# Dense filler products on TensorE in two context attentions: one per two half steps, twelve at the beginning

## The chip, the cores and the metric

The kernel runs on one core of a Trainium2 chip. The metric is the device time of one execution in microseconds; three executions give a median of 5088.73 us. The core has a matrix engine (TensorE, PE in the rows; its weight loads are PEld), VectorE (DVE), ScalarE (ACT), GpSimd (POOL) and a queue engine (SP) that issues DMAs. They run side by side and meet at semaphores.

## What is computed

A decoder of four layers over x (4 batches, 512 tokens, 128 features) and a context of 154 tokens. Each layer has a self attention, an attention to the context and a feed-forward part; after each comes a residual sum and a layer norm. The change touches the context attentions of layers 0 and 1 (16 heads of 8 features). Layer 0:

```python
Q, K, V = (proj(q, w_q), proj(k, w_k), proj(v, w_v))
scores = jnp.einsum('bhqd,bhkd->bhqk', Q, K) / jnp.sqrt(jnp.float32(D_K))
keep = (mask != 0)[:, None, None, :]
scores = jnp.where(keep, scores, NEG)
attn = jax.nn.softmax(scores, axis=-1)
x = jnp.einsum('bhqk,bhkd->bhqd', attn, V)
```

Layer 1 first picks for each query the context token with the best score, and attends over the picked tokens (a token picked several times counts as often):

```python
idx = jnp.argmax(scores, axis=-1)
mem = jnp.take_along_axis(kv, idx[..., None], axis=1)
...
attn = jax.nn.softmax(logits, axis=-1)
out = jnp.einsum('bhlm,bmd->bhld', attn, mv)
```

In the kernel the mask of the first, and the never-picked tokens of the second, are a key bias: one more row of the key stack (`key_bias`). The causal attention of layer 1 and the context attention of layer 2 use masks and no key bias, the differential attention of layer 2 neither; all go through the same function.

## The kernel before

`attend` (L496) does all heads of one attention. Its main loop has N = 32 slots, one for a pair of heads of a batch; two slots are a quad. A context attention has four half steps in a slot, numbered k = 0, 1 (outer) and i = 0, 1 (inner); a half step is also called a unit, and its place in the quad (0 to 7) decides what else is done there. Each half step has two sets of scores of one head:

- the **turned** scores (`turned`, L626; product at L635): keys on the partitions, 512 queries as columns, into one of three banks. ScalarE takes the exponential (L766).
- the **direct** scores (`direct`, L651; products at L667): queries on the partitions, two products of 154 columns, into another three banks. VectorE takes their maximum (L838). They run `AHEAD` = 4 slots before the turned ones, since the maximum has to reach the turned product as rows of its query stack.

The maxima go from VectorE to GpSimd (`split`, three bf16 pieces), to TensorE (`turn_rows`, L685), to ScalarE (`copy_rows`, L772) and by DMA on SP's queue (L598) into the stack. The turned product of a slot's first half step waits for that DMA. SP issues in order; the same queue also loads the stacks of the next batch (`load_next`).

The stacks of the two heads of a pair lie on partitions 0 to 63 and 64 to 127. A turned product uses one half, and the direct products of the same half step the other one (`e = 1 - i`).

In its order TensorE goes through `slot(n)` (L718): for each half step the turned product, the direct products of slot n + 4, and at certain places the value products (L703, four of 256 columns in fp32), the row turns (places 1 and 5) and the head transposes of the last quad (L714, place 6, after ScalarE's `copy_heads` and `copy_rows`). The last four slots have no direct products. Ahead of the slots stands a run-up of `AHEAD` slots with direct products only, 16 units in a context attention and 24 in the causal one (where `AHEAD` is 3). In the run-up each unit is followed by `keep_awake` (L671, product at L673), a product whose result nobody reads: the identity times 256 columns of the first piece of the projected queries (`q_parts`), into the bank of the value products. It is there for context and causal attentions, not for the differential one. Within the slots there is none.

VectorE begins a context attention by clearing eight buffers (L852) before its first maximum.

Of the kernel before, what the change touches and what calls it, by code (L numbers as in the profile page):

```python
# [18 lines left out]
P = 128  # L19
B, S, D = 4, 512, 128  # L20
# [475 lines left out]
def attend(nc, g, stacks, which, rows, out, context, causal=False, key_bias=None, mask=None):  # L496
# [10 lines left out]
    COLS = 32  # L507
    N, QUADS = B * PAIRS, B * PAIRS // 2
    AHEAD = 4 if context else 3
    SENT_AHEAD = 2  # L510
    max_row = stacks.max_row

# [9 lines left out]
    with ExitStack() as stack:  # L522
# [17 lines left out]
        x_bank, o_bank = g.bank[2], g.bank[7]  # L540
# [15 lines left out]
        def d_bank(n, k, i):  # L556
            return d_banks[unit(n, k, i) % 3]
# [28 lines left out]
        with nc.Block() as block:  # L586
# [25 lines left out]
            def _(pe):  # L612
# [38 lines left out]
                def direct(n, k, i):  # L651
# [10 lines left out]
                    if plain:  # L662
                        after(pe, "max_done", unit(n, k, i) - 2)
                    rows_e = slice(64 * e, 64 * e + max_row)
                    for at, q in enumerate(direct_steps[k]):
                        keys = (q + 1) * P if causal else nk
                        ins = nc.tensor.matmul(d_bank(n, k, i)[:, at * nk:at * nk + keys], q_stack[rows_e, q * P:(q + 1) * P],  # L667
                                               k_stack[rows_e, 0:keys], start=plain, stop=True, skip_group_check=True)
                    ins.then_inc(s["direct_ready"], 1)

                def keep_awake():  # L671

                    nc.tensor.matmul(o_bank[:, 0:S // 2], g.ident_bf[:, :], stacks.parts[which][0][:, 0, 0:S // 2],  # L673
                                     start=True, stop=True, skip_group_check=True)

                def free_x():
                    after(pe, "rows_done", issued["rows"])
# [40 lines left out]
                def slot(n):  # L718
                    quad = n // 2
                    ahead = n + AHEAD  # L720
                    for k in range(C):
                        for i in range(2):
# [14 lines left out]
                            if at == TURN_HEADS_AT and quad:  # L737
                                turn_heads(quad - 1)

                for n in range(AHEAD):  # L740
                    for k in range(C):
                        for i in range(2):
                            if not plain:
                                direct_masks(n, k, i)
                            direct(n, k, i)
                            if context or causal:
                                keep_awake()
                    if 0 < n <= SENT_AHEAD:
                        turn_rows(n - 1)
                for n in range(N):  # L750
# [79 lines left out]
            def _(dve):  # L830
# [20 lines left out]
                for buffer in cleared:  # L851
                    nc.vector.memset(buffer[:, :], 0.0).then_inc(s["cleared"], 1)  # L852
                for n in range(AHEAD):
                    for k in range(C):
# [2844 lines left out]
```

## Time and profile before

| | |
|---|---|
| median of three executions | 5088.73 us (5082.01 to 5094.36) |
| the profiled execution | 5093.95 us, its span 5092.2 us |
| PE busy | 3827.4 us, 75% of the span |
| DVE, ACT, POOL busy | 3247.2, 2786.9, 1400.7 us |
| first context attention (attend) | from 483 to 636 us |
| causal attention | from 831 to about 1165 us |
| second context attention with a key bias | from 1259 to 1429 us |
| context attention of layer 2 | from 2076 to about 2270 us |

TensorE's clock is granted at one of two levels, 1.2 or 2.4 GHz; the granted clock of a stretch is its mean as a share of 2.4 GHz. An engine's busy time in the profile counts matmuls from their start to a modelled end, so products that follow each other overlap; distances between starts tell what a product costs. The idle time in brackets is the engine's, before the row, with what ended it; "issue" is a wait with no releaser seen by the profile.

### The profile page before, as it was taken

How to read it: one execution, taken by the hardware profiler on the slowest of the kernel's cores; microseconds unless marked ns; L12 is line 12 of the kernel's file. 1: busy time of each engine (PE TensorE's matmuls, PEld its weight loads, DVE VectorE, ACT ScalarE, POOL GpSimd, SP SyncE). 2: the span in 40 equal slices, each digit the busy share in tenths (PEclk: the TensorE clock that was granted, in tenths of full speed). 3: DMA queues.
4: the chain of work that ended last, by engine and by line, in shares of the span. 5: the costliest groups of instructions: out<-in, count | busy, mean ns of one | idle time of the engine just before them, and what ended most of it. 6: DMA issues, size and time to landing. Idle time of an engine off the chain costs nothing. (4 is left out here: it accounts for less than half of the span.)

```text
span 5092.2 us, 96128 instructions
## 1 busy us (share of the span) xinstructions
PE 3827.4 (75%) x32913; PEld 2248.5 (44%) x33140; DVE 3247.2 (64%) x6512; ACT 2786.9 (55%) x7830; POOL 1400.7 (28%) x2146
## 2 busy tenths in 40 slices
PE   2004768996767996786997668888888888888886
PEld 1003333333342222343443336666666666666664
DVE  8996444443427786435555327777787878777775
ACT  2034623442646875451224437777777777777775
POOL 0011101011112111210000135444555545454553
PEclk6556876555777988797997679999999999999998
DMA  1001133101213310302541000000000000000000
GB/s 45 0 0 33 35 81 69 32 14 27 41 34 82 83 27 14 68 10 78 142 136 34 5 23 28 5 9 24 5 28 5 6 27 5 9 24 5 28 5 11
DMA packets 139047, 170.17 MB, mean 33 GB/s; under 512 B 34607, under 2 KB 121755, under 8 KB 137412
## 3 DMA queue, kind: packets, MB, share of 16 engines
q1 hardware_dynamic: 138158, 164.06, 13.0%
q8 instruction: 261, 4.28, 0.4%
q14 instruction: 196, 1.61, 0.1%
q0 software_dynamic: 432, 0.23, 0.0%
HBM read 124.06 MB, written 32.89 MB: 31 GB/s over the span
## 5 line engine op out<-in xcount | busy, mean ns | idle before, releaser
L838 DVE TENSOR_REDUCE minus_max<-banks 128x1 f32<-128x512 f32 (+4 forms) x1152 | 622.5, 572 | 477.5 <-PE banks L667 467.0
L766 ACT ACTIVATE probs<-banks 128x512 f32<-128x512 f32 (+4 forms) x1152 | 615.8, 559 | 436.2 <-PE banks L635 426.8
L2966 POOL TENSOR_TENSOR loc_by_query<-loc_by_query,loc_inv_sums 128x512 f32<-128x512 f32 x386 | 470.1, 1236 | 560.2 <-DVE loc_inv_sums L3372 560.2
L2959 POOL TENSOR_TENSOR loc_cos_part<-loc_cos_part,loc_sin_part 128x512 f32<-128x512 f32 x388 | 488.2, 1277 | 414.5 <-DVE loc_sin_part L3350 413.8
L3247 ACT ACTIVATE loc_by_query<-banks,loc_minus_max 128x128 f32<-128x128 f32 x1544 | 540.6, 375 | 13.6 <-DVE loc_minus_max L3387 13.1
L3015 PE MATMUL banks<-loc_w_qkv,loc_shifted 128*128 128x256 f32 x1552 | 413.6, 414 | 169.4 <-ACT loc_by_query L3247 155.1
L635 PE MATMUL banks<-q_stack,k_stack 51*128 51x512 bf16 (+4 forms) x1152 | 444.4, 430 | 35.9 <-DMA q_stack<-max_rows 34.5
L667 PE MATMUL banks<-k_stack,q_stack 48*128 48x512 bf16 (+5 forms) x1536 | 443.3, 349 | 30.7 <-PEq L68 19.7
L3015 PEld LDWEIGHTS banks<-loc_w_qkv,loc_shifted 128*128 128x128 f32 x1552 | 310.0, 205 | 282.9 <-issue 229.4
L703 PE MATMUL banks<-probs,pair_rows 128*32 128x256 f32 (+1 forms) x4352 | 398.4, 448 | 8.6 <-issue 8.6
L3347 DVE TENSOR_TENSOR loc_cos_part<-banks,loc_table 128x512 f32<-128x512 f32 x388 | 265.5, 684 | 127.6 <-ACT loc_square L3216 126.5
L3247 ACT ACTIVATION_READ_ACCUMULATOR loc_by_query<-banks,loc_minus_max 128x1 f32 x1544 | 331.5, 215 | 0.0
L3216 ACT ACTIVATE loc_square<-banks 128x512 f32<-128x512 f32 x388 | 225.5, 604 | 108.2 <-PE banks L3015 107.4
L1349 ACT ACTIVATE gated<-banks 128x512 f32<-128x512 f32 x168 | 100.3, 597 | 336.7 <-PE banks L1310 336.7
L2012 PE MATMUL banks<-identity,srt_b 128*128 128x128 f32 x64 | 11.3, 320 | 344.6 <-DVE srt_b L2283 344.6
L3379 DVE TENSOR_TENSOR loc_rotated<-loc_cos_part,loc_inv_norm 128x512 f32<-128x512 f32 x388 | 267.5, 690 | 1.1 <-issue 0.6
L3350 DVE TENSOR_TENSOR loc_sin_part<-banks,loc_table 128x512 f32<-128x512 f32 x388 | 264.4, 681 | 0.0
L206 POOL TENSOR_SCALAR fin_shifted<-fin_moments 128x4 f32<-128x4 f32 x48 | 12.0, 250 | 892.1 <-DVE fin_moments L306 889.7
L800 POOL CAST max_parts<-minus_max 128x8 bf16<-128x8 f32 x192 | 36.7, 191 | 767.9 <-DVE minus_max L838 767.9
L3359 DVE TENSOR_REDUCE loc_norm_sq<-loc_square 128x8 f32<-128x512 f32 x388 | 246.4, 677 | 0.0
L1369 DVE TENSOR_TENSOR product<-gated,banks 128x512 f32<-128x512 f32 x168 | 115.4, 687 | 199.7 <-PE banks L1312 199.6
L635 PEld LDWEIGHTS banks<-q_stack,k_stack 51*128 51x128 bf16 (+1 forms) x1152 | 101.9, 97 | 294.1 <-issue 151.1
(491 smaller groups left out, 8783.6 us busy)
## 6 DMA issues: line engine op xcount, KB each, us to landing
expert_share<-limited_rows SPq DMA_DIRECT2D x136, 256.0 KB, 4.0
expert_w<-in_L_ffn_pairs_dram SPq DMA_DIRECT2D x84, 192.0 KB, 2.4
q_stack<-q_pieces SPq DMA_DIRECT2D x38, 384.0 KB, 6.3
loc_w_qkv<-in_L_ffn_Wqkv_dram SPq DMA_DIRECT2D x7, 1536.0 KB, 6.9
expert_share<-grouped_rows SPq DMA_DIRECT2D x32, 256.0 KB, 4.1
k_stack<-k_pieces SPq DMA_DIRECT2D x20, 384.0 KB, 9.6
q_pieces<-q_parts SPq DMA_DIRECT2D x19, 384.0 KB, 2.6
q_stack<-max_rows SPq DMA_DIRECT2D x384, 3.0 KB
```

Of the source, the lines that this page charges most:

```text
L635: nc.tensor.matmul(t_bank(n, k, e)[:, q0:S], k_stack[rows_e, k0:k0 + P], q_stack[rows_e, q0:S], start=plain, stop=True, skip_group_check=T ...
L667: ins = nc.tensor.matmul(d_bank(n, k, i)[:, at * nk:at * nk + keys], q_stack[rows_e, q * P:(q + 1) * P], k_stack[rows_e, 0:keys], start=pl ...
L703: ins = nc.tensor.matmul(o_bank[at:at + COLS, lo:hi], pair_rows[quad % 2][u][:, k, e, :], probs_of(2 * quad + u, k, e)[:, lo:hi], start=(k ...
L766: nc.scalar.activation(probs_of(n, k, e)[0:kn, q0:S], t_bank(n, k, e)[0:kn, q0:S], ACT.Exp, scale=scale).then_inc(s["exp_done"], 1)
L838: nc.vector.tensor_reduce(minus_max[:, n % 2, 1 - i, qs[0]:qs[0] + len(qs)], view, AX.X, ALU.max, negate=True).then_inc(s["max_done"], 1)
L2959: nc.gpsimd.tensor_tensor(cos_part[:, tiles, :], cos_part[:, tiles, :], sin_part[:, tiles, :], ALU.add).then_inc(s["summed"], 1)
L2966: nc.gpsimd.tensor_tensor(seen, seen, inv_sums[:, h, :].unsqueeze(1).unsqueeze(3).to_broadcast([P, 2, QT, BLOCK]), ALU.mult).then_inc(s["p ...
L3015: ins = nc.tensor.matmul(g.bank[3 * j][:, (t % 2) * QK:(t % 2 + 1) * QK], xs[:, t * P:(t + 1) * P], w_qkv[:, ds(at, QK)], start=True, stop ...
L3247: nc.scalar.activation(by_query[:, h, :, t % 2, r, :], score_banks[h][:, t * 2 * BLOCK:(t + 1) * 2 * BLOCK].rearrange("p (w k) -> p w k", ...
L3347: nc.vector.tensor_tensor(cos_part[:, tiles, :], g.bank[3 * j][:, :].rearrange("p (t d) -> p t d", t=2), table[:, 0, tiles, :], ALU.mult). ...
L3350: nc.vector.tensor_tensor(sin_part[:, tiles, :].rearrange("p t (e two d) -> p (t e) two d", two=2, d=half), src, table[:, 1, tiles, :].rea ...
L3379: nc.vector.tensor_tensor(groups(rotated[:, tiles, :]), groups(cos_part[:, tiles, :]), inv_norm[:, part].unsqueeze(2).to_broadcast([P, 8, ...
```

## The change

`keep_awake` now takes a bank, and its product becomes 128 columns of the projected queries times 512 columns of them, over the whole bank, in place of the identity times 256 columns. Where there is a key bias, `direct` issues one such product into the bank of its own direct scores for every half step with i = 1, after the wait for that bank and before the direct products that overwrite it; and twelve of them stand ahead of everything else that TensorE does in `attend`. The old ones in the run-up stay, with the new product. The two attentions get 2 x (64 + 12) = 152 more products; 72 old ones (16, 24 and 16 in layers 0 and 1, 16 in layer 2) double their columns.

```diff
@@ -507,6 +507,7 @@
     AHEAD = 4 if context else 3
+    WAKING = 12
     SENT_AHEAD = 2
@@ -662,16 +663,18 @@
                     rows_e = slice(64 * e, 64 * e + max_row)
+                    if key_bias is not None and i == 1:
+                        keep_awake(d_bank(n, k, i))
                     for at, q in enumerate(direct_steps[k]):
                         keys = (q + 1) * P if causal else nk
...
-                def keep_awake():
-
-                    nc.tensor.matmul(o_bank[:, 0:S // 2], g.ident_bf[:, :], stacks.parts[which][0][:, 0, 0:S // 2],
-                                     start=True, stop=True, skip_group_check=True)
+                def keep_awake(bank):
+
+                    some = stacks.parts[which][0][:, 0, :]
+                    nc.tensor.matmul(bank[:, :], some[:, 0:P], some[:, 0:S], start=True, stop=True, skip_group_check=True)
@@ -737,6 +740,9 @@
+                if key_bias is not None:
+                    for _ in range(WAKING):
+                        keep_awake(o_bank)
                 for n in range(AHEAD):
                     for k in range(C):
                         for i in range(2):
@@ -744,7 +750,7 @@
                             direct(n, k, i)
                             if context or causal:
-                                keep_awake()
+                                keep_awake(o_bank)
```

TensorE at the beginning of the first context attention, before (L667 direct, L673 the old filler; line numbers of the changed kernel are three higher from there on):

```order
L611 UNCONDITIONAL_BRANCH
L667 MATMUL banks<-k_stack,q_stack 128x154 x2
L673 MATMUL banks<-q_parts,identity_bf 128x256
L667 MATMUL banks<-k_stack,q_stack 128x154 x2
L673 MATMUL banks<-q_parts,identity_bf 128x256
L667 MATMUL banks<-k_stack,q_stack 128x154 x2
```

and with the change (L670 direct, L677 the new filler):

```order
L612 UNCONDITIONAL_BRANCH
L677 MATMUL banks<-q_parts 128x512 x12
L670 MATMUL banks<-k_stack,q_stack 128x154 x2
L677 MATMUL banks<-q_parts 128x512 x2
L670 MATMUL banks<-k_stack,q_stack 128x154 x2
L677 MATMUL banks<-q_parts 128x512
L670 MATMUL banks<-k_stack,q_stack 128x154 x2
```

Twelve products stand ahead of the first direct ones, and two instead of one between the units with i = 0 and i = 1.

TensorE in a slot, from the head transposes (place 6) over places 7, 0 and 1 to place 2, before:

```order
L714 MATMUL banks<-identity,headsT 128x128 x4
L635 MATMUL banks<-q_stack_1,k_stack_1 128x512
L667 MATMUL banks<-k_stack_1,q_stack_1 128x154 x2
L703 MATMUL banks<-probs_1,pair_rows_1 32x256 x4
L635 MATMUL banks<-q_stack_1,k_stack_1 128x512
L667 MATMUL banks<-k_stack_1,q_stack_1 128x154 x2
L635 MATMUL banks<-q_stack_1,k_stack_1 128x512
L667 MATMUL banks<-k_stack_1,q_stack_1 128x154 x2
L703 MATMUL banks<-probs_1,pair_rows_1 32x256 x4
L685 MATMUL banks<-identity_bf,max_parts 6x128 x4
L635 MATMUL banks<-q_stack_1,k_stack_1 128x512
```

and with the change:

```order
L717 MATMUL banks<-identity,headsT 128x128 x4
L636 MATMUL banks<-q_stack_1,k_stack_1 128x512
L677 MATMUL banks<-q_parts 128x512
L670 MATMUL banks<-k_stack_1,q_stack_1 128x154 x2
L706 MATMUL banks<-probs_1,pair_rows_1 32x256 x4
L636 MATMUL banks<-q_stack_1,k_stack_1 128x512
L670 MATMUL banks<-k_stack_1,q_stack_1 128x154 x2
L636 MATMUL banks<-q_stack_1,k_stack_1 128x512
L677 MATMUL banks<-q_parts 128x512
L670 MATMUL banks<-k_stack_1,q_stack_1 128x154 x2
L706 MATMUL banks<-probs_1,pair_rows_1 32x256 x4
L688 MATMUL banks<-identity_bf,max_parts 6x128 x4
```

The filler parts the turned product of places 7 and 1 from its direct products; nothing else changes its place.

## Rows read from the trace of the kernel before

**Rows 1.** Stretches: length, busy PE, PEld, DVE, ACT, POOL (instructions), clock, DMA share, GB/s

```profile
503.16:619.65 116.49, 87.28 (x908) 37.73 (x908) 53.28 (x132) 77.09 (x148) 24.47 (x130) 0.86 0.19 38
619.65:635.50 15.85, 12.13 (x128) 4.89 (x124) 1.65 (x8) 11.20 (x22) 1.16 (x6) 1.00 0.01 3
1280.29:1405.30 125.01, 98.08 (x908) 40.79 (x908) 53.34 (x133) 77.57 (x148) 24.46 (x130) 0.76 0.19 36
1405.30:1428.50 23.20, 19.66 (x132) 6.39 (x124) 1.64 (x8) 11.41 (x22) 1.16 (x6) 0.62 0.01 2
831.40:851.70 20.30, 20.24 (x76) 6.09 (x77) 11.29 (x24) 0.59 (x1) 3.08 (x14) 0.50 0.72 147
2080.80:2095.30 14.50, 14.22 (x103) 7.92 (x104) 7.00 (x16) 1.17 (x2) 2.62 (x14) 0.50 0.46 65
```

**Rows 2.** Timeline, PE, one quad at full clock: start, us, engine, line, tiles, count

```profile
601.77 0.63 PE L714 MATMUL banks<-identity,headsT 128*128 128x128 f32 x4 [1.86 <-issue]
602.33 0.39 PE L635 MATMUL banks<-q_stack,k_stack 52*128 52x512 bf16 x1
...
602.64 0.64 PE L703 MATMUL banks<-probs,pair_rows 128*32 128x256 f32 x8
...
603.44 0.29 PE L667 MATMUL banks<-k_stack,q_stack 49*128 49x154 bf16 x2
603.67 0.64 PE L703 MATMUL banks<-probs,pair_rows 128*32 128x256 f32 x8
604.13 0.39 PE L685 MATMUL banks<-identity_bf,max_parts 128*6 128x128 bf16 x4
604.45 0.39 PE L635 MATMUL banks<-q_stack,k_stack 52*128 52x512 bf16 x1
...
609.24 0.63 PE L714 MATMUL banks<-identity,headsT 128*128 128x128 f32 x4 [1.86 <-issue]
```

**Rows 3.** Timeline, ACT, the same quad: exponentials from places 0 and 4

```profile
603.64 1.82 ACT L766 ACTIVATE probs<-banks 128x512 f32<-128x512 f32 x3 [0.30 <-PE banks L635]
...
606.64 0.60 ACT L766 ACTIVATE probs<-banks 128x512 f32<-128x512 f32 x1 [0.23 <-PE banks L635]
```

**Rows 4.** Timeline, DVE, reciprocals, one a quad: four of the first attention, two of the second

```profile
514.71 0.25 DVE L844 RECIPROCAL recip<-banks 128x16 f32<-128x16 f32 x1
...
538.60 0.25 DVE L844 RECIPROCAL recip<-banks 128x16 f32<-128x16 f32 x1
549.82 0.25 DVE L844 RECIPROCAL recip<-banks 128x16 f32<-128x16 f32 x1
...
619.65 0.25 DVE L844 RECIPROCAL recip<-banks 128x16 f32<-128x16 f32 x1
...
1292.27 0.25 DVE L844 RECIPROCAL recip<-banks 128x16 f32<-128x16 f32 x1
...
1405.27 0.25 DVE L844 RECIPROCAL recip<-banks 128x16 f32<-128x16 f32 x1
```

**Rows 5.** Timeline, PE, third context attention at full clock: mask products

```profile
2163.15 0.39 PE L623 MATMUL banks<-mask,identity_bf 128*128 128x512 bf16 x1
2163.38 0.31 PE L647 MATMUL banks<-identity_bf,mask 128*128 128x128 bf16 x4
```

**Rows 6.** Timeline, PE, beginnings: first attention to slot 1, then the second

```profile
483.06 0.41 PE L667 MATMUL banks<-k_stack,q_stack 49*128 49x154 bf16 x2 [9.87 <-PEq L68]
483.40 0.39 PE L673 MATMUL banks<-q_parts,identity_bf 128*128 128x256 bf16 x1
...
487.70 0.44 PE L667 MATMUL banks<-k_stack,q_stack 49*128 49x154 bf16 x2 [2.52 <-DVE minus_max L838]
...
497.76 0.60 PE L635 MATMUL banks<-q_stack,k_stack 52*128 52x512 bf16 x1
...
503.16 0.60 PE L635 MATMUL banks<-q_stack,k_stack 52*128 52x512 bf16 x1 [3.23 <-DMA q_stack<-max_rows]
...
1262.00 0.41 PE L667 MATMUL banks<-k_stack,q_stack 49*128 49x154 bf16 x2 [6.90 <-DMA k_stack<-key_bias]
```

## The prediction

> **What bounds the kernel now.** The page's chain of waits says nothing here, since it ends in the last sublayer, 2.8 ms behind the edits. I read the stretches of the touched attentions instead, then TensorE and ScalarE at single rows. In the first context attention the granted clock is 0.86 of full over the slots, in the second 0.76, and in the second one's last four slots 0.62, where the first has 1.00 for the same work: 23.20 us against 15.85 us [rows 1]. The clock has two levels, 1.2 and 2.4 GHz, so 0.76 is about half of the time at either. What that costs is read from the quads (two slots, eight half steps; one reciprocal each). With a full clock a quad takes 609.24 - 601.77 = 7.47 us [rows 2]. Twelve quads take 619.65 - 514.71 = 104.94 us in the first and 1405.27 - 1292.27 = 113.00 us in the second [rows 4], where 12 x 7.47 = 89.6 us would do. So the low clock and three stalls at a new batch cost 15.3 + 23.4 = 39 us in the two, and 7.35 us more in the second one's end.
>
> Who is waited for inside a full-clock quad decides the price of a filler. TensorE is idle only once, 1.86 us before the head transposes of L714 [rows 2]: they wait for ScalarE's last copy. From there to the turned product of place 4, ScalarE waits for TensorE: 0.30 us before the exponential of place 0, 0.23 us before that of place 4 [rows 3]; at place 2 the turned product starts at 604.45 and takes 0.39 us [rows 2], so it ends at 604.84, in the middle of the run of three exponentials, and I take the third of them as waiting too. TensorE is thus the path from place 7 through places 0 to 4, ScalarE from place 4 to the transposes.
>
> **The filler between turned and direct.** It stands behind the turned product of every odd place (i = 1) and ahead of the direct one. From the rows at full clock: a turned product and its direct partner use different row halves and run at once; whatever comes next starts 0.31 us after them (602.33 to 602.64) [rows 2]. With the filler this is turned to filler 0.31; filler to direct as four dense 128-column products to the next turned one, 604.13 to 604.45, 0.32; direct to next 0.23 (603.44 to 603.67) [rows 2]. Together 0.86 instead of 0.31: 0.55 us for a filler. At place 1 it is 0.54. Where two full-height products follow each other a 512-column one costs only 0.23 (2163.15 to 2163.38) [rows 5]; the rest of 0.55 is two changes between half and full height and the lost overlap with the direct product. The nearest rows bound a filler by 0.23 and 0.55; I take 0.55, since the neighbours here are half-height products.
>
> That price agrees with the Trainium skill, "TensorEngine Tiling (Array Packing)", Key Properties, by which a change of tiling mode drains the engine; its "Instruction Overhead" counts no such drain, and "TensorE: Matmul & The Clock Gate", Part 2, gives a lone 512-column product N / 2.4 + 2.5 = 216 ns, by which a quad would come to about 8.1 us. That is the cheap rival below.
>
> Of the four fillers of a quad, those of places 7, 1 and 3 lie on the path; that of place 5 is covered by the 1.86 us ahead of the transposes. VectorE and GpSimd are not late by it: the maxima they make are for four slots on. So a full-clock quad goes from 7.47 to 7.47 + 3 x 0.55 = 9.1 us. If all 24 quads had the full clock they would take 218.4 us, where they take 217.9 us now. **The filler's own time eats what the clock can give back in the slots.** At the low clock a filler on the path costs about 0.9 us (0.43 for its columns, and the direct product alone).
>
> Does the clock hold? Before, it falls after the wait of 1.86 us with little ahead of it, and in each of the three batch stalls (538.60 to 549.82 is a quad of 11.2 us, 3.7 over the full-clock one) [rows 4]. Fillers shorten the wait to about 1.86 - 0.55 = 1.3 us and fill its neighbourhood, so I expect fewer falls; the stalls are of DMA and remain: 3 x 3.7 = 11 us. Slots: 218.4 + 11 - 217.9 = +11.5 us.
>
> **The twelve at the beginning, and the wider ones.** At the low clock a 512-column product takes twice the 256-column one's stream; turned 0.60 against the old filler's 0.39 [rows 6] gives 0.21 for 256 columns, so 0.43 a filler and 5.1 us for twelve. In the first attention TensorE starts at 483.06 and goes on with unit 3 at 487.70, when VectorE has cleared its buffers [rows 6]; the twelve end at 488.2, and units 0 to 2 stand behind them now. In the second the twelve lie in the 6.90 us wait for the key bias [rows 6] but run over it by 2.5 us. The run-up of 16 units then takes, at full clock and per two units, direct 0.23, filler 0.23, filler 0.32, direct 0.23, filler 0.32, together 1.33 us; that is 10.6 us, and 0.6 for two row turns: slots begin near 499.4 instead of 497.76 [rows 6]. The first row turn is 2.0 us later, and with it everything that SP issues in order behind it: the batch load and the rows of slot 1, for which TensorE waits 3.23 us until 503.16 [rows 6]. That restart moves to 505.2. The wait stays over 3 us, so the clock gained is lost there. Slots 1 to 3 then hold four fillers on the path at mixed clock, 4 x 0.6 = 2.4 us. Entry: 2.05 + 2.4 = 4.5 us each, +9 us.
>
> The first context attention's last four slots have no filler and run at 1.00 now; the second's are entered with a higher clock and may go from 23.2 toward 15.85 us: -6 us, a full gain being 7.35 [rows 1].
>
> The old fillers of the run-up double their columns too, in the causal attention and in the third context attention, which get nothing else. TensorE is busy 20.24 of 20.30 us there and 14.22 of 14.50 us, all at clock 0.50 [rows 1], so each adds its 0.21 us: 24 x 0.21 = 5.1 us, and 13 x 0.21 = 2.8 us (three of its sixteen are ahead of VectorE's clearing). Their neighbours stay the same, so the clock there stays at 0.50 in my forecast; if the wider fillers woke it, both would gain instead.
>
> **Sum.** 11.5 + 9 - 6 + 5.1 + 2.8 = **+22 us** on the profiled execution of 5093.95 us (span 5092.2), which is 5 us above the median of the runs: 5088.73 + 22 = 5111 us.
>
> **Rivals.** *The clock never falls in the slots* (the stalls at a new batch vanish because slots are longer, and the entry is warm behind its wait): slots +0.5, entry +2.6, end -7.35, elsewhere +7.9: +4 us, 5092 us. For it: a longer quad gives the row DMA more time. Against: the wait of 3.23 us at slot 1 is longer than those of 1.86 us that the clock outlives in [rows 2], and the second attention enters its slots through the same kind of wait.
>
> *The clock gets caught low.* In that state products of half height, fillers and direct ones no longer overlap, so TensorE streams less densely after a fall than now, and recovery takes longer. A quad that is half of the time low would take near 11.3 us: 24 x 11.3 = 271, +53 in the slots, +9, -2, +8: +68 us, 5157 us. It decides if the granted clock of the slots comes out under about 0.8. For it: the second attention's 0.76 [rows 1]. Against: a filler at full height is itself dense work, and the stretch between two waits gets more of it.
>
> *Cheap fillers* (this one ends faster): 0.23 us each, 3 x 0.23 = 0.7, a quad of 8.16 us, 24 x 8.16 = 196. With the clock held: -22 + 2.6 - 7.35 + 7.9 = -19 us, 5070 us; with the stalls kept -8. It decides from a filler under about 0.4 us on the path. Against: every row where half and full height meet shows 0.1 us of change.
>
> *The clock does not rise at all from them* is part of the second rival.
>
> **How the numbers follow.** Forecast (+8 to +35) 0.42; clock never falls (-5 to +8) 0.20; caught low (+35 to +75) 0.18; cheap, or a waking of the causal attention that I did not foresee (under -8) 0.20. A measurement of this kernel can tell about 0.2%, 10 us, from no change. Slower by more than that: most of the forecast and all of the low case, 0.55; within: 0.25; faster: 0.20. The range from 5078 to 5150 takes the forecast, the never-falling case and the nearer half of the low one, about 0.75 to 0.8.
>
> **What would show it.** Full-clock quads of 9.1 us (8.2 for the cheap rival); 0.31, 0.32 and 0.23 us between turned, filler, direct and the next; a restart at slot 1 two microseconds later; granted clock of 0.9 or more in the slots of both attentions; the second one's end near 16 us; 5 us more in the causal run-up at 0.50. I am wrong if ScalarE hides the fillers, or if clock 1.00 appears in the causal attention.

## The result, and the profile after

| | before | after |
|---|---|---|
| median, run side by side | 5091.55 us (5082.01 to 5112.48) | 5205.7 us (5201.31 to 5213.61) |
| profiled span, granted clock | 5092.2 us, 0.830 | 5200.4 us, 0.821 |

The ratio is 1.0204, with a 95% interval of 1.017 to 1.0238: slower. The forecast was 5111 us with a range of 5078 to 5150. The sign is right, the size is not: +114 us by the medians, where +22 stood in the sum, and the time lies outside the range. Between the two spans it is 108.2 us.

The stretches of the kernel after that answer to [rows 1], in the same columns and the same order: the slots of the first context attention from the restart at slot 1, its last four slots, the same two of the second one, then the run-ups of the causal and of the third context attention.

```profile
507.63:670.69 163.06, 141.74 (x948) 49.65 (x962) 57.11 (x133) 78.58 (x148) 24.28 (x130) 0.68 0.13 27
670.69:690.55 19.86, 16.35 (x128) 5.66 (x124) 1.63 (x7) 11.18 (x21) 1.15 (x6) 0.74 0.01 2
1335.66:1515.40 179.74, 157.93 (x948) 53.21 (x962) 57.12 (x133) 79.35 (x148) 24.30 (x130) 0.58 0.13 25
1515.40:1532.60 17.20, 13.47 (x132) 5.15 (x124) 1.65 (x8) 11.05 (x21) 1.15 (x6) 0.93 0.01 2
889.20:910.80 21.60, 21.27 (x67) 5.25 (x66) 10.18 (x20) 0.80 (x2) 1.96 (x10) 0.50 0.58 123
2179.33:2196.60 17.27, 16.60 (x104) 7.98 (x107) 6.93 (x15) 1.17 (x2) 2.81 (x15) 0.50 0.42 61
```

The first and the third line are where the time is. The granted clock is 0.68 and 0.58 where it was 0.86 and 0.76, and the slots take 163.06 and 179.74 us instead of 116.49 and 125.01. VectorE and ScalarE have the same work to within 4 us. The ends moved as well: the first attention's last four slots lost their full clock (19.86 us instead of 15.85), the second's gained one (17.20 instead of 23.20).

One whole quad of the kernel after at full clock, from one group of head transposes to the next (PE timeline, columns as in [rows 2]; L717 head transposes, L636 turned, L677 filler, L670 direct, L706 values):

```profile
587.29 0.63 PE L717 MATMUL banks<-identity,headsT 128*128 128x128 f32 x4 [1.30 <-issue]
587.86 0.39 PE L636 MATMUL banks<-q_stack,k_stack 52*128 52x512 bf16 x1
588.17 0.39 PE L677 MATMUL banks<-q_parts 128*128 128x512 bf16 x1
588.50 0.30 PE L670 MATMUL banks<-k_stack,q_stack 49*128 49x154 bf16 x2
588.73 0.64 PE L706 MATMUL banks<-probs,pair_rows 128*32 128x256 f32 x8
...
596.44 0.63 PE L717 MATMUL banks<-identity,headsT 128*128 128x128 f32 x4 [1.30 <-issue]
```

The three distances are 0.31, 0.33 and 0.23 us, the wait before the transposes is 1.30 us, and the quad takes 596.44 - 587.29 = 9.15 us: the forecast's full-clock quad, step by step. The same work at the low clock:

```profile
655.91 1.09 PE L717 MATMUL banks<-identity,headsT 128*128 128x128 f32 x4 [1.20 <-issue]
656.93 0.61 PE L636 MATMUL banks<-q_stack,k_stack 52*128 52x512 bf16 x1
657.47 0.61 PE L677 MATMUL banks<-q_parts 128*128 128x512 bf16 x1
658.01 0.44 PE L670 MATMUL banks<-k_stack,q_stack 49*128 49x154 bf16 x2
658.38 1.08 PE L706 MATMUL banks<-probs,pair_rows 128*32 128x256 f32 x8
```

Here it is 0.54, 0.54 and 0.37 us. The transposes before these began at 641.26, so this quad took 14.65 us. VectorE's reciprocals, one a quad, show how many quads are like that; here are five in a row of the first attention:

```profile
533.85 0.25 DVE L850 RECIPROCAL recip<-banks 128x16 f32<-128x16 f32 x1
...
548.50 0.25 DVE L850 RECIPROCAL recip<-banks 128x16 f32<-128x16 f32 x1
...
563.14 0.25 DVE L850 RECIPROCAL recip<-banks 128x16 f32<-128x16 f32 x1
...
577.79 0.25 DVE L850 RECIPROCAL recip<-banks 128x16 f32<-128x16 f32 x1
...
589.23 0.25 DVE L850 RECIPROCAL recip<-banks 128x16 f32<-128x16 f32 x1
```

Three quads of 14.6 us stand side by side. Five of the first attention's twelve quads and eight of the second's have that length; before, the longest of all 24 was 11.6 us, with a batch stall in it. And this is the moment at which those three begin:

```profile
531.13 0.84 PE L717 MATMUL banks<-identity,headsT 128*128 128x128 f32 x4 [1.30 <-issue]
531.90 0.61 PE L636 MATMUL banks<-q_stack,k_stack 52*128 52x512 bf16 x1
532.44 0.61 PE L677 MATMUL banks<-q_parts 128*128 128x512 bf16 x1
```

The transposes take 0.63 us at full clock and 1.09 at the low one; 0.84 is the fall itself. It comes behind a wait of 1.30 us, with no DMA stall near, in a full-clock quad. From there to about 581 us the clock is at 0.50. Stretches of the same trace before, in and behind it:

```profile
524.00:528.00 4.00, 3.75 (x45) 1.54 (x42) 2.25 (x7) 2.63 (x5) 0.78 (x4) 1.00 0.81 256
536.00:540.00 4.00, 3.64 (x26) 1.21 (x25) 0.96 (x2) 1.48 (x4) 0.00 (x0) 0.50 0.00 0
576.00:580.00 4.00, 4.00 (x19) 0.93 (x18) 1.41 (x4) 1.65 (x3) 0.78 (x4) 0.50 0.02 6
584.00:588.00 4.00, 2.70 (x27) 1.22 (x19) 1.72 (x4) 2.50 (x5) 1.09 (x6) 1.00 0.01 4
```

That is 50 us at the low clock, with no wait in the quads longer than 1.30 us. Before, the kernel went through waits of 1.86 us at full clock [rows 2], and where the clock fell it soon rose again. Read in steps of 0.5 us, the granted clock shows 14 low stretches in the 24 quads before, 81 us together and none over 10.2 us. After, it shows only 6, but 229 us together, the longest 82 us. The falls did not become more frequent (a long stretch may of course hide some); each of them lasts far longer.

Between the traces the time goes as follows (before to after, from reciprocal to reciprocal):

| stretch | before | after | difference |
|---|---|---|---|
| start of the program to the first reciprocal | 514.71 | 523.92 | +9.2 |
| first attention, 12 quads | 104.94 | 146.77 | +41.8 |
| its last four slots | 15.85 | 19.86 | +4.0 |
| from there through the causal attention and up to the second's first reciprocal | 656.8 | 664.2 | +7.4 |
| second attention, 12 quads | 113.00 | 160.6 | +47.6 |
| its last four slots | 23.20 | 17.20 | -6.0 |
| the rest | 3663.7 | 3667.8 | +4.1 |

89 of 108 us are in the 24 quads.

### The profile page after: what moved, and what is told of

Read it like the earlier page. It is cut to its first block and busy times, and to the rows that moved or that the text cites. A ratio compares the mean times of both kernels' runs of the same rounds, so it can differ in the third digit from the quotient of the medians.

```text
span 5200.4 us, 96396 instructions
## 1 busy us (share of the span) xinstructions
PE 3953.6 (76%) x33029; PEld 2276.3 (44%) x33292; DVE 3255.0 (63%) x6512; ACT 2788.2 (54%) x7830; POOL 1398.0 (27%) x2146
## 5 line engine op out<-in xcount | busy, mean ns | idle before, releaser
L636 PE MATMUL banks<-q_stack,k_stack 51*128 51x512 bf16 (+4 forms) x1152 | 456.2, 441 | 24.8 <-DMA q_stack<-max_rows 23.4
L670 PE MATMUL banks<-k_stack,q_stack 48*128 48x512 bf16 (+5 forms) x1536 | 449.6, 352 | 22.4 <-PEq L68 9.9
L706 PE MATMUL banks<-probs,pair_rows 128*32 128x256 f32 (+1 forms) x4352 | 414.1, 464 | 9.0 <-issue 8.9
L3353 DVE TENSOR_TENSOR loc_cos_part<-banks,loc_table 128x512 f32<-128x512 f32 x388 | 265.3, 684 | 125.1 <-ACT loc_square L3222 123.6
L3222 ACT ACTIVATE loc_square<-banks 128x512 f32<-128x512 f32 x388 | 225.6, 605 | 108.7 <-PE banks L3021 108.2
L2018 PE MATMUL banks<-identity,srt_b 128*128 128x128 f32 x64 | 11.9, 333 | 344.6 <-DVE srt_b L2289 344.6
L636 PEld LDWEIGHTS banks<-q_stack,k_stack 51*128 51x128 bf16 (+1 forms) x1152 | 103.1, 98 | 296.3 <-issue 160.6
```

The lines of the kernel that those rows point to most:

```text
L636: nc.tensor.matmul(t_bank(n, k, e)[:, q0:S], k_stack[rows_e, k0:k0 + P], q_stack[rows_e, q0:S], start=plain, stop=True, skip_group_check=T ...
L706: ins = nc.tensor.matmul(o_bank[at:at + COLS, lo:hi], pair_rows[quad % 2][u][:, k, e, :], probs_of(2 * quad + u, k, e)[:, lo:hi], start=(k ...
L3353: nc.vector.tensor_tensor(cos_part[:, tiles, :], g.bank[3 * j][:, :].rearrange("p (t d) -> p t d", t=2), table[:, 0, tiles, :], ALU.mult). ...
```

## The experiments

Ratios are to the kernel before on the same chip, whose median was 5102.93 to 5110.85 beside these runs; single executions of it went from 5087.75 us at a mean clock of 0.831 to 5131.62 us at 0.821 beside e1. "12 quads" is the time from the first to the thirteenth reciprocal of the first and of the second attention, in the profiled execution; before it is 104.9 and 113.0 us, after 146.8 and 160.6.

### Which part of the change costs: e1_slots_only, e2_beginning_only

The first has the fillers of the slots alone (no twelve, old filler in the run-up); the second has all but them.

```diff
+                    if key_bias is not None and i == 1 and n >= AHEAD:
+                        dense(d_bank(n, k, i))
```

That is e1's edit of the kernel before (`dense` issues the changed kernel's filler). This is e2's edit of the changed one:

```diff
-                    if key_bias is not None and i == 1:
+                    if key_bias is not None and i == 1 and n < AHEAD:
```

> The kernel before with only the fillers of the slots: one dense 512-column product between the turned and the direct products of every odd half step (56 in each of the two attentions with a key bias), nothing at the beginning, the old fillers of the run-up unchanged everywhere. Theory A (the fillers between turned and direct keep the clock low after each fall): the slots of the two attentions lose nearly all that the full change loses there, 80 to 95 us over the kernel before, with a granted clock near 0.6 to 0.7 in them. Theory B (the beginning upsets the start, and the slots follow from there): under 40 us. Full-clock quads 9.1 us, low ones 14.7 by either.

> The changed kernel without the fillers of the slots: the twelve at the beginning, the wider ones of the run-up and the second filler of odd units there stay. Theory A: +12 to +20 us over the kernel before (entries 2 x 2 to 4, causal run-up 5, third context attention 3), the slots' clock near 0.8 as before. Theory B: 60 us or more, most of it in the slots.

e1: 5193.07 us, 1.0172 (1.0129 to 1.0215); 12 quads 152.9 and 153.6 us at clock 0.63. e2: 5122.01 us, 1.002 (0.9993 to 1.0046), not to be told from no change; 12 quads 119.6 and 109.0. The slots' fillers alone make nearly the whole loss: +82 us by the medians, inside the 80 to 95 of theory A. The first attention of e2 also shows a state of its own: a row of quads of 10.24 us each, low for a part of every quad, as the second attention of before had in its later half. So its clock there is 0.69, not the 0.8 of theory A (0.85 in the second attention).

### Is it the filler's work or its place: e3_ahead_of_turned

The changed kernel with the slots' filler ahead of the turned product, in the same bank and as often, so that turned and direct stand side by side again.

```diff
-                    if key_bias is not None and i == 1:
+                    if key_bias is not None and i == 1 and n < AHEAD:
                         keep_awake(d_bank(n, k, i))
...
+                            if key_bias is not None and i == 1 and ahead < N:
+                                after(pe, "max_done", unit(ahead, k, i) - 2)
+                                keep_awake(d_bank(ahead, k, i))
```

> The changed kernel with each filler of the slots moved ahead of the turned product of the same half step: same number, same bank, same operands, but the turned and the direct products stand side by side again. Theory A in its full form (it is the lost overlap of turned and direct products, not the number of fillers, that keeps the clock from rising): a low-clock quad of 13 us or less in place of 14.7, clock of the slots 0.75 or more, at least 40 us faster than the changed kernel. Rival C (any added product on the path costs the same, wherever it stands): within 15 us of the changed kernel's 5206.

5129.48 us, 1.0035 (1.0013 to 1.0058); 12 quads 117.7 and 125.1 us, at clock 0.87 and 0.79. The timeline around such a filler:

```profile
566.78 0.39 PE L677 MATMUL banks<-q_parts 128*128 128x512 bf16 x1
567.11 0.39 PE L636 MATMUL banks<-q_stack,k_stack 52*128 52x512 bf16 x1
567.11 0.30 PE L670 MATMUL banks<-k_stack,q_stack 49*128 49x154 bf16 x2
567.42 0.64 PE L706 MATMUL banks<-probs,pair_rows 128*32 128x256 f32 x8
```

Turned and direct start together at 567.11, and the next comes 0.31 us later; the filler costs 0.33 instead of 0.56 us, and a full-clock quad is 8.5 us. The same fillers, moved by one place, give back 1.7 of the 2.0%, and 307.4 - 242.9 = 64.5 us in the 24 quads (before, 217.9). The mean clock is that of before: these fillers neither raise nor lower it, and cost their own time. Two points fall short of theory A. The two wholly low quads, in the second attention, take 13.6 us, not 13 or less, and they lie in one low stretch of 31 us, longer than any of before. So the overlap accounts for most of the difference, not for every long stretch.

### Is the lost overlap enough: e6_same_half

The kernel before, without any filler, but with the direct product of each half step in the same row half as its turned one, so that the two can't run at once.

```diff
-                    e = 1 - i
+                    e = i if key_bias is not None else 1 - i
...
```

The cut line gives VectorE's maximum the same row half.

> No filler at all beyond those of the kernel before: in the two attentions with a key bias the direct products of a half step take the same half of the rows as its turned product, so that the two no longer run side by side. Theory A (a lower density of the stream at the low clock, from lost overlap, keeps the clock low): slots at clock 0.7 or less, +40 us or more over the kernel before. Rival (it takes the fillers themselves): clock of the slots as before, 0.76 to 0.87, and 0.2 to 0.25 us for each of four half steps on the path at full clock, a quad of 8.4 us, 20 to 35 us slower.

5151.35 us, 1.0086 (1.0058 to 1.0114). The windows over 12 quads, first attention of e6:

```profile
512.75:645.96 133.21, 118.63 (x820) 45.18 (x816) 48.89 (x122) 69.64 (x133) 22.43 (x120) 0.58 0.16 33
```

Clock 0.58, with quads of 11.9 us low and 9.2 in part; the second attention has 134.7 us at 0.56. So the slots' clock depends on the overlap of the two half-height products here. Without it, and with nothing added, the clock stays low for most of the time, though the wait before the transposes is shorter than before (1.71 us at full clock, 1.05 at the low one). Theory A asked for 0.7 or less and +40 us; it is +45 us by the medians. e6 takes the overlap from eight half steps of a quad and the change from four, so it is no measure of the change's size, but it shows the mechanism alone. TensorE is no less busy by the profile for it: 118.63 of 133.21 us is 89%.

### Is it what the filler multiplies: e7_identity

The changed kernel with the identity as the stationary operand of every filler.

```diff
-                    nc.tensor.matmul(bank[:, :], some[:, 0:P], some[:, 0:S], start=True, stop=True, skip_group_check=True)
+                    nc.tensor.matmul(bank[:, :], g.ident_bf[:, :], some[:, 0:S], start=True, stop=True, skip_group_check=True)
```

> The changed kernel with the identity as the stationary operand of every filler in place of 128 columns of the projected queries: same number, shape, bank and place. If what the filler's operand holds counts for the clock, the slots' clock differs from the 0.67 and 0.59 of the changed kernel and the time by over 15 us. If shape and place alone count, as theory A says: within 12 us of it.

5208.31 us, 1.0203 (1.0173 to 1.0234); 12 quads 156.9 us at 0.61 and 153.0 at 0.63. The same as the change. What the filler's stationary operand holds does not matter; its moving operand was the projected queries in both, so data as such are not tested.

### Elsewhere in the stretch that is waited for: e8_behind_values

The slots' fillers behind the value products (places 7, 1, 2, 3), in the next direct bank.

```diff
-                    if key_bias is not None and i == 1:
+                    if key_bias is not None and i == 1 and n < AHEAD:
...
+                            following = unit(ahead, k, i) + 1
+                            if key_bias is not None and (at in VALUES_NEXT or at in VALUES_OWN) and following < N * 2 * C:
+                                after(pe, "max_done", following - 2)
+                                keep_awake(d_banks[following % 3])
```

> The changed kernel with its four fillers of a quad moved behind the four value products (places 7, 1, 2, 3), full height behind full height, turned and direct products side by side again. By the rows of before a filler costs 0.22 us there at full clock in place of 0.55: a quad of 8.3 to 8.4 us. Theory A: denser at the low clock than the kernel before, clock of the slots 0.85 or more, 80 us faster than the changed kernel, about +5 us over the kernel before. Rival C: within 40 us of the changed kernel.

5139.6 us, 1.006 (1.0039 to 1.0081); 12 quads 124.3 and 125.3 us, both at 0.83, most of them 10.3 us long. Rival C is out, but so are theory A's numbers: 0.85, a quad of 8.3 to 8.4 us and +5 us over the kernel before, where +34 us was measured. A filler costs 0.33 us at full clock (533.10 to 533.43), not 0.22, since the product behind it is a half-height one again. The clock falls about once a quad, but no low stretch is longer than 6.8 us: with the overlap kept there are no long ones, and each filler is paid.

### In the wait itself: e4_in_the_wait, e5_waits_and_stalls

Both are made from the kernel before. e4 puts four dense products into the wait of 1.86 us ahead of the head transposes. e5 does so in the last four slots too and adds ten in each of the three batch stalls (slots 1, 11 and 19), ahead of the wait for the row DMA.

```diff
+                        if key_bias is not None and n in (1, 11, 19):
+                            after(pe, "exp_done", unit(n, k, e) - 2)
+                            for _ in range(10):
+                                dense(t_bank(n, k, e))
                         pe.wait_ge(s[f"sent{n % 2}"], 32 * (n // 2 + 1))
...
+                                if key_bias is not None:
+                                    after(pe, "max_done", min(unit(ahead, k, 1) - 2, N * 2 * C))
+                                    for _ in range(4):
+                                        dense(d_banks[unit(ahead, k, 1) % 3])
```

That is e5's edit; e4 has only the second part, and only where there are direct products ahead (`ahead < N`).

> The kernel before with four dense products per quad ahead of the head transposes, where TensorE waits 1.86 us at full clock for ScalarE, and none elsewhere. If the clock falls because of that wait, four products (0.9 us) inside it hold the clock and cost nothing at full clock: a quad stays at 7.5 us, granted clock over 0.9 in the slots, 15 to 40 us faster than the kernel before. If the falls come from the DMA stalls alone: within 10 us of it, or slower by up to 15 us, since at the low clock the four take 1.7 us of a path without that wait.

> e4_in_the_wait, with four dense products in the wait of the last four slots too, and ten of them ahead of the wait for the row DMA of slots 1, 11 and 19, where TensorE stands 3 us for the DMAs queued behind a batch load. If those stalls are what still drops the clock, the slots come to 0.97 or more, stall quads from 12 to 10.5 us, the last slots from 20 to 16 us: 8 to 20 us faster than e4_in_the_wait. If ten products lie on the path where the stall is shorter than they are: within 5 us of it.

e4: 5075.38 us, 0.9935 (0.9915 to 0.9956), clock 0.93, 12 quads 98.9 and 100.4 us. e5: 5052.14 us, 0.989 (0.9869 to 0.9912). The windows of e5: 12 quads of the first attention, its last four slots, 12 quads of the second; then one place 6 of its PE timeline:

```profile
510.38:606.39 96.01, 83.70 (x888) 36.01 (x884) 47.90 (x121) 68.54 (x133) 22.47 (x120) 1.00 0.23 46
606.39:622.24 15.85, 14.07 (x136) 5.52 (x132) 1.64 (x8) 11.20 (x22) 1.16 (x6) 1.00 0.01 3
1273.90:1370.60 96.70, 83.72 (x890) 36.01 (x886) 47.95 (x122) 68.58 (x133) 22.48 (x120) 1.00 0.23 46
```

```profile
521.67 0.39 PE L639 MATMUL banks<-q_stack,k_stack 52*128 52x512 bf16 x1
521.68 0.30 PE L671 MATMUL banks<-k_stack,q_stack 49*128 49x154 bf16 x2
521.99 1.04 PE L683 MATMUL banks<-q_parts 128*128 128x512 bf16 x4
523.92 0.63 PE L723 MATMUL banks<-identity,headsT 128*128 128x128 f32 x4 [0.89 <-issue]
```

The four products take 1.04 us of the wait and leave 0.89; the quad stays 7.48 us (516.44 to 523.92). The clock is 1.00 in both attentions from the first reciprocal through the last four slots. Fillers can hold the clock, then, where TensorE waits and the overlapping pairs are left alone. e4 came out as forecast (35 us faster than before, clock 0.93); its low stretches lie at the batch stalls. e5 is 23 us faster than e4, a little over the 8 to 20 forecast; its stall quads take 10.4 to 11.0 us.

Low stretches in the 24 quads of the profiled executions, from the granted clock in steps of 0.5 us (one that is cut by the ends of the 24 quads counts with its part):

| kernel | stretches | together, us | longest, us |
|---|---|---|---|
| before | 14 | 81 | 10.2 |
| after | 6 | 229 | 82 |
| e1, fillers of the slots alone | 8 | 225 | 51 |
| e3, fillers ahead of the pairs | 9 | 84 | 31 |
| e6, no overlap, no fillers | 7 | 230 | 65 |
| e8, fillers behind the values | 22 | 86 | 6.8 |
| e5, waits and stalls filled | 0 | 0 | |

Where the pairs overlap (before, e3, e8) all but one of these stretches end within 10.2 us; where they are parted or share a row half (after, e1, e6) most last tens of microseconds.

### The twelve, once the clock holds: e10_twelve_with_held_clock

e5 with twelve dense products at the beginning of the two attentions with a key bias.

```diff
+                if key_bias is not None:
+                    for _ in range(12):
+                        dense(o_bank)
                 for n in range(AHEAD):
```

> e5_waits_and_stalls with the twelve dense products at the beginning of the two attentions with a key bias, the run-up's old fillers unchanged: what the twelve are worth where the rest holds the clock. Mine: 5.1 us at the low clock on the path of the first, 2.5 of the second, and the run-up of 14.7 and 12.3 us shortened to 10 at the full clock: within 5 us of e5_waits_and_stalls. Rival: the run-up at the full clock also brings slot 1's rows sooner, 5 to 10 us faster.

5064.8 us, 0.9905 (0.9871 to 0.9939); 12 quads 96.3 and 100.2 us. The interval overlaps that of e5 (0.989, 0.9869 to 0.9912), so no gain or loss can be told from e5, and the rival's 5 to 10 us are not seen. The clock is at 1.00 in the slots of e5 without them.

### The causal attention: e9_causal_too, e11_longer_causal_fill

Before, the causal attention runs at the low clock throughout. A window from its first reciprocal on (its thirteenth is at 1132.35):

```profile
890.10:1146.50 256.40, 256.40 (x1572) 81.53 (x1570) 105.46 (x226) 105.08 (x243) 25.92 (x129) 0.50 0.13 24
```

TensorE is busy all 256.40 us, at 0.50. e9 is e5 and, for the causal attention, twelve dense products ahead of its run-up and ten in each of its three batch stalls. In e11 the first of these stalls gets 28.

```diff
+                def through_stall(n):
+                    if (key_bias is not None or causal) and n in (1, 11, 19):
+                        after(pe, "exp_done", unit(n, 0, 0) - 2)
+                        for _ in range(10):
+                            dense(t_bank(n, 0, 0))
...
+                if causal:
+                    for _ in range(12):
+                        dense(o_bank)
```

`through_stall(n)` now stands ahead of everything else in a slot, the masks too (e10 has it so as well). e11 differs from e9 by this:

```diff
-                        for _ in range(10):
+                        for _ in range(28 if causal and n == 1 else 10):
```

> e5_waits_and_stalls, and in the causal attention, whose slots run at clock 0.50 throughout, twelve dense products ahead of the run-up and ten ahead of the wait of slots 1, 11 and 19. If the low clock there is only a state that it never gets out of by its own stream, but would stay out of, its quads fall from 20.2 us toward the 11.2 us of the differential attention, which runs at the full clock: 80 to 110 us faster than e5_waits_and_stalls. If its stream cannot hold the full clock either: within 10 us, or 5 to 10 us slower (the added products at the low clock).

> The kernel of e9, with 28 instead of 10 dense products ahead of slot 1 of the causal attention, where that kernel's TensorE still waited 4.07 us for the row DMA and its clock then stood at 0.50 for the five quads from 850 to 945 us. Theory (the clock falls for want of dense work in that wait, and the causal slots' own work holds a clock of 1.00 once it is there): the wait shrinks to near zero, the first slots stay at 1.00, their quads take 12.3 us instead of 20.2; three such quads and two beside them give back some 35 us, to about 4945 us. Rival (the causal slots in their early part cannot hold the clock; it rose only because of the work of the later ones): the clock falls again behind slot 1 and the time stays within 10 us of 4980.

e9: 4979.72 us, 0.9736 (0.9694 to 0.9778). Two stretches of its causal attention:

```profile
876.63:937.19 60.56, 60.56 (x374) 19.30 (x372) 25.24 (x54) 24.61 (x57) 6.02 (x31) 0.50 0.32 68
956.89:1057.87 100.98, 100.42 (x1004) 42.33 (x1004) 65.57 (x146) 64.29 (x152) 15.65 (x80) 1.00 0.14 18
```

The same loop takes 20.2 us a quad in the first line and 12.3 in the second, with 2.6 us of a batch stall in the line. The clock rose in the ten products that stand ahead of slot 11, between 949 and 950 us (the granted clock is 0.50 up to 949 us and 1.00 from 950 us on; nine of the ten are in this row):

```profile
947.00 3.44 PE L679 MATMUL banks<-q_parts 128*128 128x512 bf16 x9 [0.33 <-ACT probs L786]
```

So the loop did not get there by its own stream; the fillers brought it there and it kept the clock. e9 is 72 us faster than e5 by the medians, under the 80 to 110 forecast, since the first four quads stayed low. The clock had been at 1.00 in the run-up too, but fell at slot 1, where TensorE still waited:

```profile
847.51 0.60 PE L635 MATMUL banks<-q_stack,k_stack 51*128 51x512 bf16 x1 [4.07 <-DMA q_stack<-max_rows]
```

In the profile of e11 the 28 products leave 0.26 us of that wait, and the whole of the causal attention is at full clock:

```profile
849.91 0.39 PE L635 MATMUL banks<-q_stack,k_stack 51*128 51x512 bf16 x1 [0.26 <-DMA q_stack<-max_rows]
```

```profile
867.80:1019.75 151.95, 151.88 (x1511) 63.94 (x1510) 98.35 (x217) 96.53 (x228) 23.51 (x120) 1.00 0.23 44
```

That is 151.95 us for twelve quads that take 12 x 20.2 = 242 us at the low clock. But the median is 4976.15 us, 0.9761 (0.9693 to 0.9828), with four executions of 4944.08, 4957.29, 4995.01 and 4995.16, so by the median it can't be told from e9, as its rival said (within 10 us of 4980). Two are at or near the 4945 of the first theory, two are above e9. Over the whole execution the mean granted clock of the short two is 0.870 and 0.868, of the long two 0.859 each (e9: 0.860 to 0.863), so the long two lost clock somewhere. The mechanism is shown by the profiled one, 4957.29; that it happens in every execution is not, and the slower two have no profile. Both kernels beat the one before by 2.4 to 2.6%.

## Why the prediction was wrong, point by point

- **Full-clock steps: right.** Distances of 0.31, 0.32 and 0.23 us were forecast and 0.31, 0.33 and 0.23 measured; the quad 9.1 and 9.15; the wait before the transposes 1.3 and 1.30. ScalarE did not hide the fillers. At the low clock a filler costs 0.54 + 0.54 + 0.37 - 0.54 = 0.91 us (an overlapped pair takes 0.54: 647.87 to 648.41), where "about 0.9" stood. The cheap rival is out.
- **"Does the clock hold?": this is the step that failed.** The term for the slots took 24 quads at full clock and three stalls, +11.5 us; measured is +89. "I expect fewer falls" held by count, 6 low stretches for 14. But the sum put the length of a fall at nothing, and the low time went from 81 to 229 us. The argument looked only at how often the clock falls, by the length of the wait, 1.86 to 1.3 us, and at the filler as dense work; it left out how the clock comes back. The clock fell behind a wait of 1.30 us, and stayed down. The filler takes the overlap from the pair beside it, and e6 and e3 show that this decides most of it: e6 has no filler in its slots and no overlap and a clock of 0.58, e3 has all the fillers and the overlap and a clock of 0.87 and 0.79.
- **The count of stalls: a slip.** The sum has three batch stalls of 3.7 us. The third of each attention, at slot 1, lies ahead of the first reciprocal, so the 24 quads hold four (in e5, at full clock, quads of 10.86, 10.41, 10.89 and 11.02 us). That is under 4 us.
- **The rival "caught low" had the mechanism and the wrong price.** It named the lost overlap, and its mark, a clock under 0.8 in the slots, came true (0.68, 0.58). It put a quad at 11.3 us by assuming it half low. A wholly low quad is 14.65 us and they come in rows; the mean quad was 146.8 / 12 = 12.2 and 160.6 / 12 = 13.4 us. The rows read before had no wholly low quad to price it from; "half of the time low" was a guess. The 18% it got and the range that stopped halfway into it were both too small. The evidence against it ("a filler at full height is itself dense work") did not hold at this place: in e1 the fillers of the slots alone bring the clock to 0.63.
- **Entry: mechanism right, a little short.** +4.5 us for each was forecast. The first attention's TensorE work begins 485.70 - 483.06 = 2.6 us later; nothing that TensorE does ahead of it was changed (over the other runs this start lies between 480.57 and 485.97 us). Then the restart at slot 1 stands 507.63 - 485.70 = 21.9 us behind it instead of 20.1: +1.8, forecast +2.05, behind a wait of 3.39 us where over 3 was said. From there to the first reciprocal 16.3 us instead of 11.6: +4.7 for 2.4, because 10 of these us are at the low clock, where it was about 5 before. So +6.6, and +6.9 between the causal attention's end and the second's first reciprocal. "The clock gained is lost there" held: after the restart the turned products take 0.60 us again.
- **Run-ups elsewhere: right, but in the causal attention not all of it was paid.** The third context attention's takes 17.27 us for 14.50, +2.8 as forecast. In the causal one the run-up ends 910.81 - 884.60 = 26.2 us behind its first product, instead of 852.55 - 831.46 = 21.1: +5.1 as forecast, at 0.50 as forecast. Slot 1 no longer waits the 1.35 us that it waited before for its row DMA, and from its first product to its last reciprocal the causal attention takes 342.2 us instead of 339.7, so the sum's 5.1 came to 2.5.
- **The second attention's end: -6.0 for -6, by luck.** The forecast's reason was a higher clock at its entry. It was entered at the low clock (the quads before it end in a low stretch from 1483 us on), which rose at 1518 us and held. The first attention's end, forecast as unchanged, was entered at full clock, fell at 678 us behind a wait of 1.99 us and lost 4.0 us; before, it had kept the full clock through the same wait.
- **The twelve: nothing that can be measured.** e10 adds them alone, and e2 has them with the rest of the beginning; neither can be told from the kernel without. They did bring the first attention's run-up to full clock (from 490 to 507 us), which the wait at slot 1 lost again.
- **A waking of the causal attention** was named only as a way to be wrong. The wider filler did not do it; e9 and e11 show that it was there to be had, and that it is worth more than all the rest.

What stays open: why e11 has two lengths, and why the clock comes back soon when the pairs overlap and mostly takes tens of microseconds when they don't. The runs show that it does so, not why.

## What to carry to other kernels

Price a filler at both clocks and by what it does to its neighbours: between two products that run at once on different row halves it costs its own time and their overlap, and here the clock came back quickly only with the overlap. Count how long the clock stays low, not only how often it falls. Put fillers into TensorE's measured waits, where four of them left the quad at 7.5 us, and into the stalls; with both filled the clock stayed at 1.00. Lengthen them until the wait behind them is short. A stage that is 100% busy at half the clock deserves the first look: it can be the same stage at full clock, brought there once and not dropped at its first stall.

## What the runs showed of the hardware

- Busy time does not tell which clock a stage gets. TensorE was busy for 87% of the time both in twelve quads of e5 (83.70 of 96.01 us, clock 1.00) and in the first attention's slots of the kernel after (141.74 of 163.06 us, clock 0.68).
- The same causal loop sits at 0.50 for 256.40 us if it begins there, and holds 1.00 for 151.95 us if it begins there (profiled execution of e11): it keeps either level. In e9 ten fillers moved it from one to the other in the middle. I had taken a stage that never rose for one that could not. The Trainium skill, "TensorE: Matmul & The Clock Gate", Part 1, lets the clock follow from how busy TensorE has been of late; by busy time as the profile counts it, these two rows (100% of the window in both) speak against that.
- One wait of 1.30 us was followed by 50 us at the low clock (531 to 581), in slots in which a filler parts the pairs. With the pairs side by side the 14 low stretches before last 10.2 us at most.
- Moving a filler by one place, from behind the turned product to ahead of it, changed its price at full clock from 0.56 to 0.33 us and the 24 quads by 64.5 us. The lost overlap behind the first price answers to the Trainium skill, "TensorEngine Tiling (Array Packing)", Key Properties, by which different tiles can work in parallel: turned and direct start together at 567.11 in e3.
